# One-hots of lookups and of dst picks: two ScalarE activations where VectorE made one wide compare

## The reference

```python
# gcn_conv, twice (weights W1, b1, relu; then W2, b2, sigmoid), with self-loops
dinv = rsqrt(segment_sum(ew, dst))
out  = segment_sum((x @ W)[src] * (dinv[src] * ew * dinv[dst])[:, None], dst) + b
x = layernorm(x + gcn(x))
# attention
z, rh = h @ fc_w.T, r_h @ fc_r_w.T
e = leaky_relu(z[src] @ aw[0] + z[dst] @ aw[1] + rh @ aw[2])
alpha = softmax of e over the edges of one dst
out = relu(segment_sum(alpha * (z[src] + rh), dst) + z @ loop_w)
x = layernorm(x + out)
```

## Time and profile before

| | |
|---|---|
| median of 3 runs | 2682.67 us (2680.21 to 2683.11) |
| the profiled execution | 2688.04 us, span 2686.2 us |
| TensorE busy | 1962.5 us, 73% |
| VectorE busy | 1731.3 us, 64% |
| ScalarE busy | 253.3 us, 9% |
| GpSimd busy | 1998.3 us, 74% |
| mean granted TensorE clock | 0.813 |

### The profile page before, as it was taken

One profiled execution on the slowest core, in us unless ns is written; L12 is line 12 of the kernel. 1 busy time (PEld: TensorE's weight loads), 2 busy tenths in 40 slices (PEclk: granted clock), 3 DMA queues, 4 the chain that ended last, 5 costly groups with the idle time before them and its releaser, 6 DMA issues.

```text
span 2686.2 us, 39490 instructions
## 1 busy us (share of the span) xinstructions
PE 1962.5 (73%) x13505; PEld 1689.4 (63%) x13505; DVE 1731.3 (64%) x7072; ACT 253.3 (9%) x444; POOL 1998.3 (74%) x1973
## 2 busy tenths in 40 slices
PE   5777888989896787979797884466457566567558
PEld 4567767777785565757575763366456556456557
DVE  8989976867764456665656564556556457556465
ACT  0010000101100011101111111000000000000000
POOL 7777777777776777777777774777777777777772
PEclk9659888989986889889878885678788777788777
DMA  4243222222224233343424334644444444444441
GB/s 133 57 118 96 64 70 65 77 63 77 69 65 126 63 83 115 89 123 91 117 78 116 89 107 138 173 116 114 106 113 114 103 114 106 113 114 106 103 104 33
DMA packets 251443, 263.33 MB, mean 98 GB/s; under 512 B 41630, under 2 KB 195765, under 8 KB 251222
## 3 DMA queue, kind: packets, MB, share of 16 engines
q0 software_dynamic: 62784, 130.31, 19.8%
q1 hardware_dynamic: 175214, 123.97, 15.8%
q10 hardware_dynamic: 13240, 6.45, 0.8%
HBM read 247.25 MB, written 13.72 MB: 97 GB/s over the span
## 4 chain that ended last, share of the span: by engine, by line
POOL 45%; issue 19%; PE 16%; DVE 11%; DMA 7%; SPq 1%; ACT 0%; POOLq 0%; DVEq 0%; ACTq 0%
POOL ring L562 45%; PE ps L694 7%; DMA ring<-x_d,srcC 5%; DVE SR L1226 5%; PE ps L749 5%; DVE SR L1257 2%; PE ps L697 1%; DMA ring<-h_d,srcC 1%; PE ps L737 1%; DMA U<-dlo_d 1%; PE ps L679 1%; SPq L400 1%; SPq L482 1%; PE ps L634 0%; DVE SR L1323 0%
## 5 line engine op out<-in xcount | busy, mean ns | idle before, releaser
L562 POOL DMA_INDIRECT ring<-x_d,srcC x1260 | 1262.1, 1002 | 411.4 <-issue 395.2
L694 PE MATMUL ps<-SR,ring 128*128 128x128 f32 (+9 forms) x5076 | 904.3, 311 | 203.1 <-DVE SR L1257 75.3
L694 PEld LDWEIGHTS ps<-SR,ring 128*128 128x128 f32 x5076 | 797.9, 227 | 231.8 <-issue 140.5
L562 POOL DMA_INDIRECT ring<-h_d,srcC x558 | 593.5, 1064 | 183.1 <-issue 175.5
L749 PE MATMUL ps<-SR 128*128 128x376 f32 x1176 | 430.2, 518 | 33.6 <-ACT SR L989 33.6
L697 PE MATMUL ps<-SR 128*128 128x128 f32 (+10 forms) x1948 | 427.4, 305 | 0.0
L697 PEld LDWEIGHTS ps<-SR 128*128 128x128 f32 x1948 | 348.8, 224 | 0.0
L749 PEld LDWEIGHTS ps<-SR 128*128 128x128 f32 x1176 | 233.5, 207 | 176.1 <-ACT SR L989 35.4
L1323 DVE TENSOR_SCALAR SR<-iota_s,cols 128x376 f32<-128x376 f32 x588 | 246.7, 473 | 67.8 <-PE ps L749 67.5
L1257 DVE TENSOR_SCALAR SR<-iota_s,rankC,ewC 128x128 f32<-128x128 f32 x1036 | 280.0, 363 | 0.3
L829 PE MATMUL ps<-ident,cols 128*32 128x128 f32 (+2 forms) x78 | 20.4, 396 | 316.5 <-DVE cols L1533 316.5
(11 more groups left out here) (226 smaller groups left out, 1721.3 us busy)
## 6 DMA issues: line engine op xcount, KB each, us to landing
SR<-in_edge_attr_dram SPq DMA_DIRECT2D x97, 512.0 KB, 4.2
U<-dlo_d SPq DMA_DIRECT2D x98, 256.0 KB, 3.5
ring<-x_d,srcC POOLq DMA_INDIRECT x1260
SR<-low_d SPq DMA_DIRECT2D x72, 256.0 KB, 3.3
ring<-h_d,srcC POOLq DMA_INDIRECT x558
U<-lo_d SPq DMA_DIRECT2D x18, 256.0 KB, 3.2
x_d<-U SPq DMA_DIRECT2D x12, 264.0 KB, 4.5
rows<-x_d SPq DMA_DIRECT2D x12, 264.0 KB
```

Source lines behind the costliest of these rows:

```text
L562: pool.indirect_dma_start(ring[:, gg % R, k, 0:width], None, (x if p == 0 and h < R0 else table)[:, :], bass.IndirectOffsetOnAxis(ap=srcC[ ...
L694: last = nc.tensor.matmul(ps[(p * NK + k) % 2][:, lo:hi], ring[:, gg % R, j, 0:D], S[:, gg % NS, j, w0:w0 + hi - lo], start=False, stop=t ...
```

## The change

ScalarE makes both kinds of one-hot. From the low bits, in place, it takes the absolute value of the difference to the partition's number (`Abs` with the bias column -p), waits for its own result, and then takes `Relu(1 - distance)`: one where the distance is zero, zero where it is one or more. `slot_onehot` stands in ScalarE's loops behind the copies of the group and, in layer 2, before `evacuate`; `begin_pick` is moved from the end of VectorE's group to the end of ScalarE's. VectorE keeps the slot matrices and `end_pick`. Since VectorE's queue no longer orders the node table before the picks, a semaphore `table_made` does, and `make_slots` waits once a set for `unpacked`. The evacuation of the last bank but one is moved into the loop. The last 15 picks are begun by ScalarE after the last `squash`.

```diff
--- before.py
+++ after.py
@@ -197,6 +197,7 @@
         ones = sb("ones", [P, P])
         zero_h = sb("zero_h", [P, BW], BF16)
         epsc = sb("epsc", [P, 1])
+        negp = sb("negp", [P, 2])
         flag = sb("flag", [1, 1], I32)
         odd = sb("odd", [P, 4])
 
@@ -772,6 +773,8 @@
                 if q >= 2:
                     pe.wait_ge(s("picked"), q - 1)
                 k = next(k for k in range(NK) if q * GT in node_tiles(k))
+                if q * GT == node_tiles(k)[0]:
+                    pe.wait_ge(s("table_made"), k + 1)
                 for j in range(GT):
                     last = nc.tensor.matmul(ps[6 + q % 2][:, 3 * j:3 * j + 3], ohD[:, q % 2, j * P:(j + 1) * P],
                                             tabD[:, k % 2, q * GT - node_tiles(k)[0] + j, :], start=True, stop=True)
@@ -988,6 +991,29 @@
                 n = len(buckets(m)) * P
                 nc.scalar.copy(rowX[:, m % 2, 0:n], ps[3 + m % 2][:, 0:n]).then_inc(s("looked_copied"), 1)
 
+            apart = [0]
+
+            def one_hot(out, low):
+
+                apart[0] += 1
+                nc.scalar.activation(low, low, ACT.Abs, bias=negp[:, 0:1]).then_inc(s("low_apart"), 1)
+                act.wait_ge(s("low_apart"), apart[0])
+                return nc.scalar.activation(out, low, ACT.Relu, bias=negp[:, 1:2], scale=-1.0)
+
+            def slot_onehot(m):
+                n = m // NC * NL + m % NC // 2
+                c, w = m % NC % 2 * BW, len(buckets(m)) * P
+                act.wait_ge(low_loaded[n % 2], 16 * (n // 2 + 1))
+                if m >= 2:
+                    act.wait_ge(s("looked"), m - 1)
+                one_hot(ohS[:, m % 2, 0:w], loS[:, n % 2, c:c + w]).then_inc(s("oh_made"), 1)
+
+            def begin_pick(q):
+                act.wait_ge(lo_loaded[q % 2], 16 * (R0 // 2 + q // 2 + 1))
+                if q >= 2:
+                    act.wait_ge(s("pick_summed"), q - 1)
+                one_hot(ohD[:, q % 2, :], dloB[:, q % 2, :]).then_inc(s("ohd_made"), 1)
+
             def copy_set(i):
                 act.wait_ge(s("slot_summed"), NB * (i + 1))
                 if i >= 2:
@@ -1012,6 +1038,8 @@
             act.wait_ge(s("x1_stored"), 16 * 7)
             for h in range(HS[0]):
                 set_copies(0, h)
+                for m in chunks_at(0, h):
+                    slot_onehot(m)
                 for s_, g in made_at(h, 3):
                     if g == ST // GT - 1:
                         store_low(s_)
@@ -1036,12 +1064,18 @@
                     if CLOSEH[1][k] == h - 2:
                         squash(k)
                 set_copies(1, h)
-                for k in range(NK - 2):
+                for m in chunks_at(1, h):
+                    slot_onehot(m)
+                for k in range(NK - 1):
                     if CLOSEH[1][k] == h:
                         evacuate(1, k)
-            for k in (NK - 2, NK - 1):
-                evacuate(1, k)
-                squash(k)
+                for q in picks_at(h):
+                    begin_pick(q)
+            squash(NK - 2)
+            evacuate(1, NK - 1)
+            squash(NK - 1)
+            for q in range(picks_at(HS[1] - 1)[-1] + 1, G):
+                begin_pick(q)
 
             def span(r):
                 return slice(place(r[0]) * P, (place(r[-1]) + 1) * P)
@@ -1174,6 +1208,8 @@
             v.memset(ones_h[:, :], 1.0)
             v.tensor_scalar(before[:, :], iota_h[:, :], pidx[:, 0:1], None, ALU.is_gt)
             v.memset(epsc[:, :], EPS)
+            v.tensor_scalar(negp[:, 0:1], pidx[:, 0:1], -1.0, None, ALU.mult)
+            v.memset(negp[:, 1:2], 1.0)
             v.memset(rows[:, :, D:XW], 0.0)
             v.memset(padI[:, 0:DOFF], -1)
             v.memset(padI[:, DOFF:DOFF + DLEN - DOFF - E], int(FAR))
@@ -1310,12 +1346,9 @@
                 v.tensor_tensor(odd[:, 3:4], odd[:, 3:4], most[:, 0:1], ALU.max).then_inc(s("odd_found"), 1)
 
             def make_slots(m):
-                i, n_ = m // NC, m // NC * NL + m % NC // 2
-                dve.wait_ge(low_loaded[n_ % 2], 16 * (n_ // 2 + 1))
-                if m >= 2:
-                    dve.wait_ge(s("looked"), m - 1)
-                c, w_ = m % NC % 2 * BW, len(buckets(m)) * P
-                v.tensor_scalar(ohS[:, m % 2, 0:w_], loS[:, n_ % 2, c:c + w_], pidx[:, 0:1], None, ALU.is_equal).then_inc(s("oh_made"), 1)
+                i = m // NC
+                if m % NC == 0:
+                    dve.wait_ge(s("unpacked"), RUNS[i] + 1)
                 for a in buckets(m):
                     n = i * NB + a
                     if n >= NQ:
@@ -1443,12 +1476,7 @@
                 link(v.tensor_copy(tab[:, :, 1], left))
                 link(v.tensor_tensor(left, left, tab[:, :, 1], ALU.subtract))
                 link(v.tensor_copy(tab[:, :, 2], left))
-
-            def begin_pick(q):
-                dve.wait_ge(lo_loaded[q % 2], 16 * (R0 // 2 + q // 2 + 1))
-                if q >= 2:
-                    dve.wait_ge(s("pick_summed"), q - 1)
-                v.tensor_scalar(ohD[:, q % 2, :], dloB[:, q % 2, :], pidx[:, 0:1], None, ALU.is_equal).then_inc(s("ohd_made"), 1)
+                dve.sem_inc(s("table_made"), 1)
 
             def end_pick(q):
                 n = len(tiles(q))
@@ -1476,8 +1504,6 @@
                         normal(k)
                         dst_scores(k)
                         node_table(k)
-                for q in picks_at(h):
-                    begin_pick(q)
             for k in range(NK):
                 if CLOSEH[1][k] > HS[1] - 3:
                     hidden2(k)
@@ -1493,17 +1519,11 @@
                 if CLOSEH[1][k] > HS[1] - 4:
                     if rest < node_tiles(k)[0] // GT:
                         for q in range(rest, node_tiles(k)[0] // GT):
-                            begin_pick(q)
-                            if q > rest:
-                                end_pick(q - 1)
-                        end_pick(q)
+                            end_pick(q)
                         rest = node_tiles(k)[0] // GT
                     node_table(k)
             for q in range(rest, G):
-                begin_pick(q)
-                if q > rest:
-                    end_pick(q - 1)
-            end_pick(G - 1)
+                end_pick(q)
             dve.wait_ge(s("picked"), G)
             dve.wait_ge(s("set_added"), len(RUNS))
             v.memset(eC[:, 0:1], 0.0)
```

## The result

| | before | after |
|---|---|---|
| median, us | 2681.46 (2676.89 to 2686.48, 6 runs) | 2699.07 (2691.18 to 2706.44, 6 runs) |
| ratio | 1 | 1.0066, 95% interval 1.0047 to 1.0086 |
| profiled execution, us | 2688.04, span 2686.2 | 2699.6, span 2697.6 |
| VectorE busy, us | 1731.3 | 1641.1 |
| ScalarE busy, us | 253.3 | 670.1 |

The change makes the kernel slower: 17.6 us between the medians, 11.6 us between the two profiled executions.

A forecast was written before the change was run, and what follows sets the result against it. Bound: gather pace and TensorE's lag at layer ends, in layer 2 set by a ring of hand-overs. Holds 67.5 less 35, 2 and 5 gave +25.5 us: 2713.5 profiled, 2708 median; own range 2690 to 2730, overall 2665 to 2740.

The forecast's parts named there:

- likeliest case: The forecast itself: a slower kernel at 2708 us, own range 2690 to 2730, chance 0.62.
- Item 1: Layer 2, groups 19, 28, 38, 66: picks wait behind the finished set's copy, 8.2 or 5.3 us each, 27 us.
- Item 2: Layer 2, groups looking up one chunk while two are made: picks wait behind copies and one-hots on ScalarE, 16 us.
- Items 3 and 4: Layer 2: one-hots and picks behind squash, 8 us; picks behind evacuation when banks close, 7.5 us including the layer's end.
- item 4: Closing banks, layer 2: five at 0.3 us, groups 12 and 68 at 2.5 and 2.7, last sigmoid 0.8; sum 7.5.
- item 5: Layer 2: TensorE's matmuls run slower after the four long set-copy waits, 2.2 us each, 9 us added.
- the signs: Expected in the profile: layer 2 row waits near zero, pick waits for ScalarE 40 us or more, gathers at 1.30 or below.
- Case C: Rival, slower than forecast: extra ScalarE table loads for Abs (2739 us) or late dlo loads (about 2738); chance 0.12.
- What came back: Layer 2 gains: row waits 15 us, picks no longer behind node tables 10, earlier statistics and S 10; sum 35.
- share rule: Layer 1: gather gain sized by the compares' part of VectorE's busy time, 32 of 494 us, giving 3 us.
- A: Rival, faster: the gathers' pace is the bound; 2636 us, or 2655 with 20 us of holds left; chance 0.14.
- B: Rival, no change: holds at 45 us and gains at 50, giving 2678 us; chance 0.12.

The follow-up runs named there:

- e5: Changed kernel with layer 2's picks on ScalarE ahead of the set copy and the look-up one-hots: 2682.09 us, ratio 1.0004 to the kernel before.
- e6: Changed kernel with only the copy of a finished set moved behind the one-hots and picks in layer 2: 2683.02 us, ratio 1.0001 to the kernel before.
- e8: Changed kernel with the one-hots of the last 15 picks made by VectorE, one compare each: 3638.06 us on a slow chip, ratio 1.0135 to the kernel before.

## Why the prediction held

Forecast 2708, measured 2699.07, inside the likeliest case's own range (2690 to 2730). Difference to the kernel before: +25.5 forecast, +17.6 by the medians, +11.4 by the spans of the two traces. The way and the cause were right: picks wait on ScalarE behind work that has nothing to do with them, and e5 and e6 take the loss away by order alone. That the sum came so near is in part luck, as its terms, put to the stages, show:

| us | forecast | found |
|---|---|---|
| layer 1 | -5 | -0.35 |
| start of layer 2, to the sums of group 13 (pace -2, group 12 +2.5) | +0.5 | +6.8 |
| body (items 1, 2, 3, five banks of item 4, item 5, less 35) | +26.5 | -4.9 |
| end of layer 2 (item 4: 2.7 and 0.8) | +3.5 | +5.4 |
| attention stage | 0 | +4.5 |

The body, for which the forecast had all of its loss, is shorter than before. It was put 31 us too high, and the other stages together 17 us too low. By step:

**The bound.** Right. The gathers came early and the layer ended late, so TensorE's lag decided. The last sums of layer 2 start 37.6 us after its last gather (1637.56 and 1599.97) where it was 14.8 (1633.64 and 1618.84), as forecast (30 or more). TensorE waits for no rows, and the waits for picks are 41.8 us, as the signs had it. But the gathers were to come at 1.30 us or below, and came at 1.335.

**Price of an activation.** Groups of ScalarE after by line and shape, against the earlier trace rows:

```profile
L1001 ACT ACTIVATE U<-U,negp 128x1024 bf16<-128x1024 bf16 x98 | 112.5, 1148 | 3.2
...
L1001 ACT ACTIVATE SR<-SR,negp 128x512 f32<-128x512 bf16 x144 | 103.9, 722 | 4.7
```

1.15 and 0.72 us against 1.16 and 0.73. A pick one-hot follows another after 2.22 us (1094.77 to 1096.99 above), not 2.35; the next begins before the last has ended. The Trainium skill, "ScalarE: Activation LUTs", section What ACT_TABLE_LOAD costs, gave 2.27 for the pair; here the trace is slightly below it. Case C is out: the table loads of sigmoid and root are 13 and 13 in the whole trace, as many as before, and for late dlo loads ScalarE waits 11.2 us in all, where C had some 30 us of loss.

**Item 1, copies of finished sets.** Right in place, and in what TensorE waits. After, it waited for the picks' one-hots in groups 19 and 38 for 5.52 and 1.84 us, in 28 and 66 for 2.79 and 1.85: 24.0 us against 27 (7.4 and 4.6 where 8.2 and 5.3 stood). The price in time is less sure: with these waits gone in e6 the medians fall by 15.1 us, the body by 8.6.

**Item 2, one look-up while two one-hots are made.** Right. In group 53 the second pick came late:

```profile
1466.18 2.69 PE L750 MATMUL ps<-SR 128*128 128x376 f32 x8
1468.70 0.34 PE L779 MATMUL ps<-U 128*128 128x3 bf16 x8
1470.82 0.35 PE L779 MATMUL ps<-U 128*128 128x3 bf16 x8 [1.77 <-ACT U L1001]
```

Groups 16, 40, 42 and 53 waited 7.1 us together (8.8 forecast), 25, 49 and 61 another 2.5 (3.3), 29 waited 0.5 (3.1) and 18 not at all (0.8). Group 51, not in the forecast, waited 1.8. That makes 11.9 us for 16.

**Items 3 and 4 inside the body.** Too large: of the groups behind a normalisation, for which 8 us stood, 14 alone waited for picks, 1.6 us; of the five groups that close a bank, for which 1.5 us stood, none did. So the holds inside the body are 37.5 us of waiting for picks where 52.5 stood.

**Start of layer 2.** The forecast had 2 us of gain in pace here; 6.8 were lost. The sums of group 12 already began 3.5 us later, counted from the first gather (1003.19 and 1000.08), 2.3 of them at the first rows of the layer. Group 12 then waited 2.2 us for picks (2.5 forecast); behind it sixteen L738 took 3.51 us, 1.5 more than before. Why the first rows came later is open.

**Item 4 at the layer's end was under-sized.** It stood at 3.5 us (2.7 for group 68 and 0.8 for the picks before the last sigmoid) and is 5.4. TensorE after:

```profile
1637.56 2.93 PE L695 MATMUL ps<-SR,ring 128*128 128x128 f32 x12 [1.81 <-DVE SR L1293]
...
1645.61 0.80 PE L768 MATMUL ps<-w,Lb 128*128 128x128 f32 x2 [4.12 <-ACT Lb L975]
```

and before:

```profile
1633.64 2.93 PE L694 MATMUL ps<-SR,ring 128*128 128x128 f32 x12 [1.81 <-DVE SR L1257]
...
1638.66 0.49 PE L767 MATMUL ps<-w,Lb 128*128 128x128 f32 x2 [1.69 <-ACT Lb L972]
```

8.05 us from the last sums to the last product, where it was 5.02: the picks' four activations put off the sigmoid (L1058), and the last evacuation stands behind it. That is 3.0 us for the 0.8. The other 2.3 us lie one step earlier, where the two picks of group 68 stand between the product of L768 and the last sums; there 2.7 had been forecast. The forecast of 0.8 did not follow the chain of sigmoid, root and evacuation behind the one-hots.

**Item 5, slow matmuls behind a long wait.** Right in group 19 (16 L738 took 3.76 us behind the wait in group 19, 2.90 in e5), wrong as a term, and by its sign: it was added at 9 us, and the matmuls of the body take 14.1 us less. This is the largest miss of the sum. The old waits for rows and copies shrank, and slow matmuls behind them were not counted as a gain: a term counted on one side only. That this makes the 14.1 us is argued and not shown: in the body of e5 TensorE waits 94.6 us, less than the 111.5 after, and its matmuls take 499.6 us, more than the 495.2 after.

**What came back.** Waits for rows fell by 15.1 us, as forecast. The wait for pick one-hots behind a node table (9.7) is gone too, and that for copies is 9.0 us less (37.8 and 28.8). But TensorE waits 3.1 us longer for S tiles, where 20 had been counted on for earlier ones: S is built behind the reduction of the picks (end_pick), which waited 251.2 us for them in 1005 to 1640 in place of 184.5. The holds moved S with them. In all 30.7 us of waiting came back in the body where 35 stood; the sizes of the parts were wrong, and they made up for each other.

**Layer 1.** 5 us forecast, 0.35 found. VectorE was busy 18 us less there (494.04 and 475.71) and the gathers' pace stayed; the share rule gave 3, my value 7. The same layer 1 ended 3 us later in e5 and e6, so the 0.35 is no more than no change. In the body of layer 2 a gather took 453.42/434 = 1.045 us of GpSimd in place of 476.91/440 = 1.084, 17 us in all, while VectorE was busy 58 us less (378.35 and 320.05). The Trainium skill, "SBUF — State Buffer", section SBUF: two separate sides, has VectorE's two-port modes lock GpSimd out; the traces agree in kind in layer 2, but the relief is three tenths of the busy time taken away there and nil in layer 1. Part of the reason is a reading of the earlier trace rows that was wrong: it called L1323 slot compares, and took the long gather beside them for the price of what is moved. L1323 makes the slot matrices, which stay on VectorE (L1356 after). In group 53 after, GpSimd and VectorE:

```profile
1463.55 3.88 POOL L563 DMA_INDIRECT ring<-h_d,srcC  x1 [0.30 <-issue]
```

```profile
1464.15 3.17 DVE L1356 TENSOR_SCALAR SR<-iota_s,cols 128x376 f32<-128x376 f32 x8
```

A gather takes 3.88 us beside eight slot matrices, with no compare left.

**Attention stage.** The first sums started 16.2 us late (1717.7 to 1733.9): 7.0 by the layer and 9.2 by the last picks, for which 12 stood. By its group 12 only 7.1 us were left (transposes L829 at 1812.21 before, L832 at 1819.30 after): the late start cost nothing, as forecast, and e8 agrees. Yet the stage took 4.5 us longer from its first gather (1044.4), also in e5 (1045.9) and e6 (1042.7). Most of it lies behind the last gather: the end follows that gather after 47.1 us before, 50.8 after, 52.3 in e5 and 49.1 in e6. The code of this stage is the same in all four kernels, the last picks apart, and the three changed ones differ by 3.2 us among themselves. The cause is not settled, nor are the 6 us by which the medians differ more than the profiled executions; single executions of the kernel before lay between 2668.44 and 2688.51 us beside e5 and e6.

**The rivals.** A (pace is the bound) is out: the last gather of layer 2 came 18.9 us earlier where A took 40 us for the layer, and the time rose all the same. B (holds 45, gains 50) described the balance inside the body well (-4.9 us), but not its two ends. By the traces the body of e5 is 17.4 us shorter than before and that of the changed kernel 12.5 us longer than that of e5: both the gains and the holds are smaller than B's and the forecast's. The version that repairs the order only equals the kernel before.

## What to carry to other kernels

Before work is moved to an idle engine, write down that engine's queue in order and ask of each instruction what it waits for: a copy that waits for the end of a phase holds everything behind it, even if the engine is idle three quarters of the time. Here moving such copies behind the picks made the difference, by the medians, between 0.66% slower and no change. Look also at what the busy engine keeps: the operations left behind can be the ones that do the harm. If an edit moves waits from one place to another, count what follows the waits on both sides, and walk through the last groups of a stage by themselves, since no later work hides them.

## What the runs showed of the hardware

- The freed VectorE time was worth little to the gathers: 17 us for 58 us less of it in the body of layer 2, nothing for 18 us in layer 1.
- What held a gather longest is not what was moved: 3.88 us beside eight slot matrices of 128x376 alone, 0.94 us undisturbed.
- Matmuls can run slower behind waits much shorter than those of the earlier trace rows, but such a wait alone does not settle it: in the changed kernel sixteen L738 took 3.51 us behind waits of 0.37 and 1.87 us in group 12, 3.66 us behind 1.78 us in group 16, and 2.03 us behind 1.77 us in group 53.
- Three chips had stretches in which TensorE issued one matmul in 2.1 to 3.5 us for no wait that the profile shows, some 800 us in all, and every kernel took a third longer. The order of e5 and e6, which cost nothing on the faster chip (1.0004 and 1.0001), was 0.55% and 1.15% slower than the kernel before there.
